# A post-LN decoder layer on one core: last self-attention items reordered, GpSimd normalises in one operation and splits query rows, last FFN weight tile made during cross-attention

## The reference

```python
def _L0_attn_ref(x, W_K, W_Q, W_V, W_O):          # 16 heads of 128, causal
    k = jnp.einsum('ihd,bpd->biph', W_K, x)
    q = jnp.einsum('ihd,bpd->biph', W_Q, x)
    v = jnp.einsum('ihd,bpd->biph', W_V, x)
    scores = jnp.einsum('biph,biqh->biqp', k, q)
    ...
    attn = jax.nn.softmax(masked / jnp.sqrt(jnp.float32(d_head)), axis=-1)
    z = jnp.einsum('biqp,biph->biqh', attn, v)
    ...
    out = jnp.einsum('df,bqf->bqd', W_O, z_flat)
...
xq = activation_quant(rms_norm(x))                 # FFN, weights W_g, W_u, W_d as signs
g = jax.nn.silu(ternary_matmul(xq, W_g))
u = ternary_matmul(xq, W_u)
return ternary_matmul(g * u, W_d)
...
x = _layernorm(x + _L0_attn_ref(x, ...), axis=-1)
x = _layernorm(x + _L0_xattn_ref(x, ctx, ctx, gamma), axis=-1)   # 8 heads of 64 rows
x = _layernorm(x + _L0_ffn_ref(x, ...), axis=-1)
```

## Time and profile before

| | us |
|---|---|
| median of 3 runs | 1445.02 |
| lowest and highest | 1444.38, 1447.54 |
| the profiled execution's own time | 1445.03 |
| its span, first to last instruction | 1443.1 |
| PE busy | 1403.4 (97%) |
| DVE busy | 1113.6 (77%) |
| ACT busy | 701.3 (49%) |
| POOL busy | 655.3 (45%) |
| mean granted TensorE clock | 0.994 |

### The profile page before, as it was taken

One profiled execution on the slowest core, in us unless ns is written; L12 is line 12 of the kernel. 1 busy time (PEld: TensorE's weight loads), 2 busy tenths in 40 slices (PEclk: granted clock), 3 DMA queues, 4 the chain that ended last, 5 costly groups with the idle time before them and its releaser, 6 DMA issues.

```text
span 1443.1 us, 23688 instructions
## 1 busy us (share of the span) xinstructions
PE 1403.4 (97%) x6784; PEld 1146.1 (79%) x6784; DVE 1113.6 (77%) x2413; ACT 701.3 (49%) x1512; POOL 655.3 (45%) x523
## 2 busy tenths in 40 slices
PE   8899999999999999999999999979999999999998
PEld 7788888888888888888888888867888886655665
DVE  5677777877777777777787777778899877698846
ACT  3544445454444444454535444437888774333333
POOL 1434435244252543434524425255678783343434
PEclk9999999999999999999999999999999999999999
DMA  7476766757667667676675766776767944101101
GB/s 208 137 204 174 207 181 184 198 175 195 198 169 201 170 187 204 174 207 174 189 196 177 194 196 164 192 192 158 176 152 181 234 112 139 37 2 66 37 30 59
DMA packets 243885, 231.90 MB, mean 161 GB/s; under 512 B 102272, under 2 KB 212864, under 8 KB 243840
## 3 DMA queue, kind: packets, MB, share of 16 engines
q1 hardware_dynamic: 242688, 230.83, 58.3%
q10 hardware_dynamic: 1152, 0.52, 0.2%
HBM read 133.17 MB, written 90.24 MB: 155 GB/s over the span
## 4 chain that ended last, share of the span: by engine, by line
issue 44%; POOL 23%; PE 17%; DVE 7%; DMA 3%; ACT 2%; SPq 2%; POOLq 1%; DVEq 0%; ACTq 0%
POOL pT_lo L505 8%; PE bank L1653 7%; PE bank L1641 6%; POOL v_lo L503 5%; DMA xs<-rows_pair 2%; POOL xprobs L1116 2%; POOL ctx_halves L151 1%; POOL wqT_lo L498 1%; POOL wvT_lo L498 1%; DVE xpT_lo L1298 1%; DVE xneg_max L1291 1%; PE bank L1213 1%; ACT xprobs L1239 1%; PE bank L548 1%; PE bank L1173 1%
## 5 line engine op out<-in xcount | busy, mean ns | idle before, releaser
L690 ACT ACTIVATE probs<-probs,neg_max 128x128 f32<-128x128 f32 (+3 forms) x256 | 142.0, 556 | 379.5 <-DVE neg_max L819 379.5
L503 POOL TENSOR_TENSOR v_lo<-placed,v_hi 128x512 fp32r<-128x512 f32 x63 | 81.8, 1299 | 349.4 <-ACT v_hi L696 349.4
L505 POOL TENSOR_TENSOR pT_lo<-placed,pT_hi 128x1280 fp32r<-128x1280 f32 x63 | 186.3, 2958 | 0.0
L879 DVE SCALAR_TENSOR_TENSOR acc<-bank,prob_recip,acc 128x512 f32<-128x512 f32 x256 | 174.7, 745 | 5.5 <-PE bank L589 0.6
L1609 POOL TENSOR_TENSOR prod_lo<-prod,prod_hi 128x512 fp32r<-128x512 f32 x64 | 85.2, 1331 | 131.4 <-ACT prod_hi L1691 131.4
L831 DVE STREAM_TRANSPOSE turned<-probs 128x256 f32<-128x256 f32 (+1 forms) x384 | 113.9, 361 | 0.0
L789 DVE TENSOR_TENSOR qT_lo<-bank,qT_hi 128x512 fp32r<-128x512 f32 x64 | 44.2, 690 | 89.2 <-ACT qT_hi L678 89.2
L1116 POOL TENSOR_SCALAR xprobs<-xprobs,xprob_recip 128x512 f32<-128x512 f32 x128 | 86.6, 697 | 57.1 <-DVE xprob_recip L1302 57.1
L1653 PE MATMUL bank<-wdT_f32r,prod_hi 128*128 128x512 f32 x256 | 111.6, 436 | 0.8 <-POOL prod_lo L1609 0.6
L1239 ACT ACTIVATE xprobs<-bank,xneg_max 128x512 f32<-128x512 f32 x128 | 88.3, 690 | 43.3 <-DVE xneg_max L1291 40.3
L1213 PE MATMUL bank<-xpT_hi,values 128*128 128x512 f32 x256 | 103.3, 404 | 0.2 <-DVE xpT_lo L1298 0.2
(11 more groups left out here) (161 smaller groups left out, 3767.9 us busy)
## 6 DMA issues: line engine op xcount, KB each, us to landing
turned_scratch<-turned SPq DMA_DIRECT2D x64, 896.0 KB, 3.8
placed<-turned_scratch SPq DMA_DIRECT2D x252, 224.0 KB, 4.2
cp<-context_halves SPq DMA_DIRECT2D x64, 256.0 KB, 4.1
context_halves<-ctx_halves SPq DMA_DIRECT2D x16, 512.0 KB, 5.7
context_turned<-ctx_turned_block SPq DMA_DIRECT2D x32, 256.0 KB, 4.6
values<-context_turned SPq DMA_DIRECT2D x128, 64.0 KB, 2.3
xs<-rows_pair SPq DMA_DIRECT2D x60, 128.0 KB, 3.7
acc<-in_x_dram SPq DMA_DIRECT2D x16, 256.0 KB, 5.0
```

The lines of the kernel that those rows point to most:

```text
L503: nc.gpsimd.tensor_tensor(v[par][1][:], landed_values(landing), v[par][0][:].bitcast(F32), ALU.subtract).then_inc(v_lo, 1)
L505: nc.gpsimd.tensor_tensor(pT[par][1][:], landed_probs(landing), pT[par][0][:].bitcast(F32), ALU.subtract).then_inc(p_lo, 1)
L690: nc.scalar.activation(probs[:, cols], probs[:, cols], ACT.Exp, bias=low[:, par, t:t + 1], scale=-1.0, accum_out=total[:, par, t:t + 1]).t ...
L879: nc.vector.scalar_tensor_tensor(out=acc[:, b * NT + t, :], in0=s_bank[t][:], scalar=recip[:, b, t:t + 1], in1=acc[:, b * NT + t, :], op0= ...
```

## The change

- **Start.** ACT's `halves_hi(0, 0)`, which waits for the first `placed`, moves behind the casts of k of item 2 and of x tiles 12 and 13.
- **End of self-attention.** SP no longer loads the last FFN weight tiles between the exchanges of items C and D. ACT casts zT of item B before `halves_hi` of item C. DVE adds item B and splits zT of item C before the statistics of batch 0. PE makes four units of cross scores ahead of item D's output product, and DVE four row maxima.
- **The first normalisation.** POOL computes minus the mean, the reciprocal root and a shift for tile 0 (`first_norm`), ACT applies tile 0 with one activation, POOL applies tiles 1 to 3.
- **SP at the start of cross-attention.** The items' loads of `cp` and `xs` come before the values' loads, and the last tiles of the three FFN weights are loaded into the buffers of wk, wq and wv, behind them.
- **In the cross-attention.** DVE turns, ACT signs and SP keeps these three tiles at the end of the steps of heads 1, 3 and 5 of batch 0. POOL applies the normalisation (`apply_gpsimd`: add, then multiply), writes the high part of the query rows (`queries`), and `apply_beside` has one operation instead of two. `round_beside` adds -ROUND instead of subtracting ROUND.
- The helpers for the FFN tiles move into the class `Signs`, the constant `ones` shrinks from 128 to 4 columns.

```diff
+    def turn(self, nc, dve, m, h, raw):
+        dve.wait_ge(self.signed, h * 3 + m + 1)
+        dve.wait_ge(self.raw_loaded[m], h * (16 * self.E) + 16 * self.E)
+        out = self.turned[:]
+        if m < 2:
+            out = out.rearrange("p (a c s) -> p a c s", a=self.E, c=NC)
+            raw = raw.rearrange("p (a r c) -> p a c r", a=self.E, c=NC)
+        nc.vector.transpose(out, raw).then_inc(self.turn_done, 1)
+    def sign(self, nc, act, m, h):
+        act.wait_ge(self.turn_done, h * 3 + (m + 2))
+        act.wait_ge(self.kept, h * 48 + 1)
+        if m < 2:
+            out = self.gu_tile[m][:].rearrange("p c (a s) -> p c a s", a=self.E)
+            x = self.turned[:].rearrange("p (a c s) -> p c a s", a=self.E, c=NC)
+        else:
+            out, x = self.d_tile[:], self.turned[:]
+        nc.scalar.activation(out, x, ACT.Sign).then_inc(self.signed, 1)
...
+def norm_whole_gpsimd(nc, pool, norm, minus_half, n):
+    pool.wait_ge(norm.var_ready, n + 1)
+    nc.gpsimd.tensor_scalar(norm.minus_mean[:], norm.mv[:, :, 0], -1.0, 1.0, ALU.mult, ALU.mult).then_inc(norm.mean_ready, 1)
+    norm_gpsimd(nc, pool, norm, minus_half, n)
+def apply_gpsimd(nc, pool, norm, x, out, t, n):
+    if t == 0:
+        pool.wait_ge(norm.mean_ready, n + 1)
+        pool.wait_ge(norm.rstd_ready, n + 1)
+    return nc.gpsimd.tensor_scalar(out, x, norm.minus_mean[:, t:t + 1], norm.rstd[:, t:t + 1], ALU.add, ALU.mult)
...
-        loads(H - 1, 0, False)
-        exchange(FIRST + 2, 0, lambda: loads(H - 1, 1, False), landing=1)
-        loads(H - 1, 2, False)
+        exchange(FIRST + 2, 0, landing=1)
         exchange(FIRST + 3, 1)
-        keep_signs(H - 1, 0)
         sp.wait_ge(v_full, ITEMS)
         for item in range(2):
             rows.load_halves(sp, cross.cp, 0, item)
         cross.first_values(sp)
-        for m in (1, 2):
-            keep_signs(H - 1, m)
         rows.load_gamma(sp)
         cross.begin_sync(sp)
         rows.keep_halves(sp, halves, k, H - 1)
+        for m, name in enumerate(("wk", "wq", "wv")):
+            sp.wait_ge(w_turn[name], H)
+            signs.load_raw(sp, m, H - 1, raw[name][:])
         sp.wait_ge(o_added, H * B * NT)
...
         halves_lo(FIRST + 2, 0, 1)
-        norm_gpsimd(nc, pool, norm, k.minus_half, 0)
+        cross.first_norm(pool)
         halves_lo(FIRST + 3, 1)
...
         for unit in range(3):
             cross.scores(pe, unit)
+        pe.wait_ge(z_lo, ITEMS + 1)
+        cross.scores(pe, 3)
         output_product(FIRST + 3, 1)
-        for unit in range(3, 8):
+        for unit in range(4, 8):
...
+                if n == 13:
+                    halves_hi(0, 0)
...
-                if n == 1:
-                    halves_hi(0, 0)
...
-        sign(H - 1, 0)
         exps(FIRST + 3, 3)
         z_hi_of(0)
+        z_hi_of(1)
         halves_hi(FIRST + 2, 0, 1)
-        z_hi_of(1)
-        sign(H - 1, 1)
-        sign(H - 1, 2)
         z_hi_of(2)
         halves_hi(FIRST + 3, 1)
...
-        turn_ffn("wg", H - 1, 0)
         turn_v(FIRST + 3, 1)
         rows_of_scores(FIRST + 3, 3)
         turn_probs(FIRST + 3, 1)
         z_lo_of(0)
-        turn_ffn("wu", H - 1, 1)
         z_lo_of(1)
         add_outputs(FIRST, 0)
-        turn_ffn("wd", H - 1, 2)
+        add_outputs(FIRST + 1, 1)
+        z_lo_of(2)
         dve.wait_ge(o_added, (FIRST + 1) * NT)
         norm_stats(nc, dve, k, norm, norm_tiles(acc, 0), LN_EPS, 0, first=True)
-        add_outputs(FIRST + 1, 1)
-        z_lo_of(2)
         cross.first_queries_lo(dve)
-        for t in range(1, NT):
-            cross.apply_norm(dve, 0, t)
         add_outputs(FIRST + 2, 2)
         z_lo_of(3)
-        for unit in range(3):
+        for unit in range(4):
             cross.row_max(dve, unit)
         add_outputs(FIRST + 3, 3)
...
-        for pair in range(1, PAIRS):
-            source.load_values(sp, val, 0, pair)
         for h in (2, 3):
             sp.wait_ge(scores_full, (h - 1) * NT)
             load_item(sp, 0, h)
             load_queries(sp, 0, h)
+            source.load_values(sp, val, 0, h - 1)
+        source.load_values(sp, val, 0, PAIRS - 1)
...
+            if b == 0 and h - 1 in LAST_SIGNS:
+                signs.keep(sp, k, LAST_SIGNS.index(h - 1), H - 1)
...
+    def first_norm(pool):
+        norm_whole_gpsimd(nc, pool, norm1, k.minus_half, 0)
+        pool.wait_ge(norm1.rstd_ready, 1)
+        nc.gpsimd.tensor_scalar(first_shift[:], norm1.mv[:, 0, 0:1], norm1.rstd[:, 0:1], -1.0, ALU.mult, ALU.mult).then_inc(first_shifted, 1)
...
+    def apply_norm(pool, b, t):
+        apply_gpsimd(nc, pool, norm1, tile_of(b, t), tile_of(b, t), t, b).then_inc(applied, 1)
+    def queries(pool, b, pair):
+        if b * PAIRS + pair > 1:
+            for i in range(2):
+                pool.wait_ge(xs_loaded[i], 32 * (b * PAIRS + pair - 1))
+        pool.wait_ge(applied, b * NT + pair)
+        nc.gpsimd.tensor_scalar(x_parts[:, 0, :].bitcast(F32R), tile_of(b, pair), 1.0, 1.0, ALU.mult, ALU.mult).then_inc(x_hi, 1)
+        pool.wait_ge(x_hi, b * PAIRS + pair)
...
-        queries_lo(pool, 0, 1)
+        pool.wait_ge(norm1.mean_ready, 1)
+        for t in range(1, NT):
+            apply_norm(pool, 0, t)
+        queries(pool, 0, 1)
         normalise(pool, 0, 0)
         normalise(pool, 1, 1)
-        norm_gpsimd(nc, pool, norm1, k.minus_half, 1)
-        pool.wait_ge(norm1.rstd_ready, 2)
+        norm_whole_gpsimd(nc, pool, norm1, k.minus_half, 1)
...
-                queries_lo(pool, nb, nh // 2)
+                queries(pool, nb, nh // 2)
             if is_item(b, h, 1, 1):
                 quant.clear_steps(pool)
             if exists(m + 2, ITEMS):
                 normalise(pool, m + 2, (h + 2) % 4)
+            if h < NT and exists(b + 1, B):
+                apply_norm(pool, b + 1, h)
...
+        act.wait_ge(first_shifted, 1)
+        nc.scalar.activation(acc[:, 0, :], acc[:, 0, :], ACT.Identity, bias=first_shift[:], scale=norm1.rstd[:, 0:1]).then_inc(first_applied, 1)
...
+            if b == 0 and h in LAST_SIGNS:
+                signs.sign(nc, act, LAST_SIGNS.index(h), H - 1)
...
-                if j == 1 and h < NT and exists(b + 1, B):
-                    dve.wait_ge(norm1.rstd_ready, b + 2)
-                    apply_norm(dve, b + 1, h)
+                m = LAST_SIGNS.index(h)
+                signs.turn(nc, dve, m, H - 1, source.nat[m][:])
...
-        x = out(0, t)
-        if t == 0:
-            pool.wait_ge(norm.rstd_ready, 1)
-        self.nc.gpsimd.tensor_scalar(x, self.normed(0, t), norm.mv[:, t, 0:1], 1.0, ALU.subtract, ALU.mult).then_inc(self.beside_half, 1)
-        pool.wait_ge(self.beside_half, stage * NT + t + 1)
-        self.nc.gpsimd.tensor_scalar(x, x, norm.rstd[:, t:t + 1], 1.0, ALU.mult, ALU.mult
-                                     ).then_inc(norm.done if t == NT - 1 else self.beside_done, 1)
+        apply_gpsimd(self.nc, pool, norm, self.normed(0, t), out(0, t), t, 0).then_inc(norm.done if t == NT - 1 else self.beside_done, 1)
...
-        pool.wait_ge(self.beside_half, 2 * NT + t + 1)
-        self.nc.gpsimd.tensor_scalar(self.xq[:, t, :], self.scaled[:, t, :], ROUND, 127.0, ALU.subtract, ALU.min
+        pool.wait_ge(self.beside_half, t + 1)
+        self.nc.gpsimd.tensor_scalar(self.xq[:, t, :], self.scaled[:, t, :], -ROUND, 127.0, ALU.add, ALU.min
```

130 lines of the change are left out of this document (52 added, 78 removed).

## The result

The changed kernel takes **1453.43 us** (median of 22 runs, 1449.85 to 1458.03), the kernel before 1446.17 in the same runs (22, 1443.02 to 1452.80). The ratio is **1.0048, with a 95% interval of 1.0038 to 1.0058**: 7 us slower. I had forecast 1440.5, with 1447.0 as the end of the range, so both the time and the sign are wrong. The profiled execution is one of 1453.44 us, with a span of 1451.4.

What follows compares the result with a forecast made beforehand. PE, busy 97% of the span, was taken to bound the kernel. -4.7 - 3.3 + 6.8 + 1.6 - 8.5 + 3.5 = -4.6 against 1445.03 gave 1440.5 us, range 1433.5 to 1447.0.

Steps and rivals of the forecast that it cites:

- Start, -4.7: Start of self-attention: item 2's scores come at 46.0 instead of 50.70, and the whole 4.7 us gain stays.
- Last items, -3.3: End of self-attention: the reordered last items bring PE's first transposes at 979.8 rather than 983.08, 3.3 us less.
- The rule on SBUF: Last items: DVE's two query splits would wait for POOL's pT_lo, making the fourth unit some 0.5 us later.
- Item 4's loads, +6.8 and +1.6: Early cross-attention: unit 16's scores wait for xs behind SP's queue, 6.8 us idle plus 1.6 for the lower clock.
- T: End of the fourth unit's scores, 971.6, when item 2's loads start; item 4's data were due at T + 29.1.
- The rest of the cross-attention, -8.5: Units 16 to 127: GpSimd's part removes small waits, 8.5 us less, with bounds of -1 and -11.
- POOL's pair is ... 11.3 us at most: Cross-attention: POOL's work for a pair of items falls from 13.6 us to at most 11.3, against 12.8 available.
- the 13.1 us: Cross-attention to unit 127: 111 steps took 191.1 us against 178.0 at the early pace, read as many small waits.
- no idle time over 1 us up to 1130: Sign in the changed profile: no PE idle time over 1 us between 1070 and 1130, in the old time.
- The weight tiles, +3.5: End of three cross-attention steps: ACT waits for DVE's turn and signs, 3.5 us more, with bounds of 0 and +5.
- the third, small waits that stay: Rival for the cross-attention: only 3 us come back, xs waits for a longer POOL chain; 1447.0 us, chance 0.19.
- the steps from unit 16 to 127 take more than 188 us: Cross-attention: a stated sign that the forecast is wrong, if these steps take more than 188 us.

Runs made afterwards that it cites:

- experiment 8: Changed kernel with item 4's loads first and kept signs loaded over two batches, plus GpSimd splitting item D before the norm: 1439.33 us.
- experiment 2: Changed kernel with SP's order altered: FFN weights and pair 1's values loaded earlier, last pair's values behind item 4's loads: 1439.96 us.
- experiment 11: Kernel before with only GpSimd's cross-attention part: one-operation normalisation, later batches' norm and query rows' high part on GpSimd: 1444.90 us, 0.9992.
- Experiments 13 and 14: 13: kernel before plus kept signs loaded over two batches and rounding without clamp, 1444.06 us; 14: the same plus GpSimd's part, 1440.75 us.
- experiment 6: Changed kernel with item 4's loads first and kept signs over two batches, plus ACT signing weight tiles a step later: 1433.04 us.
- experiment 3: Changed kernel with the kept signs loaded in every second step of two batches instead of every step of one: 1450.35 us, 1.0026.

## Why the prediction was wrong

- **Start, -4.7: right.** 5.0 us in the trace, 5 in the run alone.
- **Last items, -3.3: right, by the trace (2.9 us; no run has this term alone).** The first transposes were forecast at 979.8 - 4.7 = 975.1 and came at 975.18; the idle time before item D's values product was to be 6 us and is 5.85. ACT's application was hidden.
- **The rule on SBUF: mechanism right, price nothing.** The first of DVE's two query splits starts at 958.38, during POOL's pT_lo (958.03 to 960.91), and takes 3076 ns, the second, beside the normalisations that follow on POOL, 1151. In experiment 8, where pT_lo is over, they take 685 and 1068; so the trace agrees with the rule of the Trainium skill, SBUF — State Buffer, "SBUF: two separate sides", that one of the two waits for the other. But DVE was done at 962.6 while PE was at D's values product from 961.06 on, so PE did not wait, and the 0.5 us were not due.
- **Item 4's loads, +6.8 and +1.6: right mechanism, size too small.** Unit 16 was due where I said (989.2 forecast, 989.1 measured), and the data came 2.6 us later. T was 0.75 late; item 4's last xs was issued at T + 27.35, not T + 25.2 (the terms ahead of it add up to 23.2, not 23.3), since the three FFN tiles took 6.6 us instead of 5.6, pairs of values 4.1 to 4.3 instead of 4.0. With the clock it is 11.7 us instead of 8.4 (units 12 to 20, against experiment 2). I had the full chain of DMAs in view and priced it from rows in which the queue was less loaded.
- **The rest of the cross-attention, -8.5: this is the step that failed.** The chip gives 1.2 for it (experiment 11), at the edge of my bounds of -1 and -11, and in the stretch from unit 16 to 127 nothing that the profile shows. Three things were wrong in "POOL's pair is ... 11.3 us at most" and in "I count 8.5 of the 13.1 us back". *First*, the rounding. I had it fall with the subtraction, and it is the min that costs: a pair with two roundings is 13.9 us of POOL for 12.8 of PE, longer than before by the 0.62 us high part, and where the kernel before waits 0.38 us for POOL, once, there are now 1.13 and 1.37. *Second*, the 13.1 us were a difference to the best pace, not a sum of waits. The view of waits has 7.1 us in the kernel before, 5.9 of them for ACT and POOL. *Third*, who is late next: xs, which is issued behind POOL's low part and then lands late while the DMA engines are full (3.44 us at 1127.67 in the changed kernel, where I had forecast no idle time over 1 us up to 1130). Experiments 13 and 14 put this into numbers: with a fast rounding and the sign loads spread the part is worth 3 to 4 us, and both together 6 to 7 against the kernel before. So most of the 8.5 hung on a rounding and a load that the kernel does not have; what holds the rest of the 13.1 us is open.
- **The weight tiles, +3.5: right, a little small.** 5.3 us (experiment 6), where I allowed 5.

The sum with the measured sizes is -5.0 - 2.9 + 13 + 5.3 - 1.2 = +9.2; the run shows +7.3 (1453.43 - 1446.17). As I read it the parts overlap: item 4's 13 us hold some of the wait for xs at 1127.67, which belongs to the loads of the signs. Of the rivals the third, small waits that stay, named the right place, and in part the right reasons (xs behind a longer POOL chain, weight tiles at 4.5 us), and gave 1447.0. Between my sum, -4.6, and the +7.3 of the run lie 11.9 us: 4.6 of item 4's loads, 7.3 of GpSimd's part and 1.8 of the weight tiles, less the overlap. What would have shown me wrong, "the steps from unit 16 to 127 take more than 188 us", did: 198.0.

Open: PE's last idle times around items C and D (5.85 and 3.0 us in the changed kernel). Three orders of POOL and DVE there gave the same time. An order with the fifth row maximum ahead of item D's add wasn't tried.

## What to carry to other kernels

When work is moved out of a loop to a later stage, write down the queue that issues its loads from the first instruction that waits to the one that is needed, and look for a gap in front of the wait: here 13 us hung on twelve loads of weights and eight of values that stood behind 12.9 us in which their queue was idle, instead of in them, and on eight more of values that could follow the needed load. A loss computed as "time less the best pace" is no stock of gains; take the view that adds up the waits, and for each ask what is late next. That view is no full account either (1.0 us less of waits and 3.3 us less of time, from experiment 13 to 14), so a run with the part alone decides. And an operation that only hands over (here 0.6 us of sign) belongs a step behind what it waits for, not right behind it.

## What was not expected of the hardware

- On GpSimd, with 128x512 f32 in: multiply-multiply and multiply-add 620 to 702 ns, add-multiply with two per-tile scalars 776, subtract-multiply 2011, add-min 1925, subtract-min 1921. Both subtract and min alone make the operation about 2 us; multiply and add do not, and the bf16 output adds nothing.
- A DMA of xs, 128 KB, landed 3.9 us (median) after its issue in the kernel before from 975 to 1040 us, and 5.7 in the changed kernel from 1108 to 1128, where each step also loads two sign tiles; with half of these loads it was 3.3 to 3.9 (experiment 3). The sign tiles alone do not explain it: the kernel before loads them there too, and xs landed after 3.8 from 1105 to 1122. What else makes the difference is not shown.
